# Squares made in the matmul slots, every second linear step on ScalarE, and the second half of an expert's weights prepared in its third slot

## The reference

```
ln(v)  = (v - mean(v)) / sqrt(var(v) + 1e-5)
si, sj = ctx @ W[:D], ctx @ W[D:]                       # one number per token each
x1     = x + tanh(g_xattn) * (0.6*sigmoid(si[:,None] + sj[None,:] + b) + 0.4*ln(x))
logits = ln(x1) @ wg                                    # 4096 tokens, 8 experts
e      = argmax(softmax(logits)); gate = softmax(logits)[e]
out    = x1 + tanh(g_ffn) * gate * (W[e] @ ln(x1) + b[e])
```

## Time and profile before

| | |
|---|---|
| median of three runs | 585.31 us |
| profiled execution, its own time | 590.49 us |
| its span | 588.7 us |
| granted TensorE clock, mean | 0.959 |
| PE / PEld / DVE / ACT / POOL busy | 538.2 / 448.9 / 406.4 / 277.3 / 336.1 us |
| first product of slot 0 | 160.16 us |
| first product of slot 2 | 188.09 us |
| last finish begins | 575.59 us |

### The profile page before, as it was taken

One profiled execution on the slowest core, in us unless ns is written; L12 is line 12 of the kernel. 1 busy time (PEld: TensorE's weight loads), 2 busy tenths in 40 slices (PEclk: granted clock), 3 DMA queues, 4 the chain that ended last, 5 costly groups with the idle time before them and its releaser, 6 DMA issues.

```text
span 588.7 us, 13585 instructions
## 1 busy us (share of the span) xinstructions
PE 538.2 (91%) x2770; PEld 448.9 (76%) x2771; DVE 406.4 (69%) x534; ACT 277.3 (47%) x408; POOL 336.1 (57%) x502
## 2 busy tenths in 40 slices
PE   8999988687797979989989999999999999999990
PEld 7888877576666858868868888888888888888880
DVE  1868858796898878946964895895598469733420
ACT  4689888688623434423433443443344234332220
POOL 2688888988743544456347336436644663474652
PEclk9699989899999989989989999999999999999996
DMA  7979885964987898786887689789678858564431
GB/s 258 384 250 264 289 313 176 334 214 154 360 318 179 249 270 224 238 242 204 251 249 240 180 241 256 224 242 257 221 221 236 260 154 243 145 212 144 139 117 36
DMA packets 84397, 135.21 MB, mean 230 GB/s; under 512 B 12048, under 2 KB 64784, under 8 KB 84368
## 3 DMA queue, kind: packets, MB, share of 16 engines
q1 hardware_dynamic: 68432, 81.88, 49.3%
q0 software_dynamic: 9792, 33.82, 15.3%
q10 hardware_dynamic: 6144, 19.18, 10.4%
HBM read 101.01 MB, written 35.93 MB: 233 GB/s over the span
## 4 chain that ended last, share of the span: by engine, by line
PE 52%; POOL 13%; DVE 12%; issue 10%; DMA 7%; ACT 2%; DVEq 1%; ACTq 1%; POOLq 1%; SPq 0%
PE pair L1265 47%; POOL table L544 5%; DVE wt L945 4%; POOL ln_b L530 2%; DVE pair L940 2%; DMA out_x<-rows,scatter_row 2%; PE pair L1199 2%; POOL xr_first L536 2%; DMA gates<-in_L_xattn_b 2%; PE pair L1187 2%; DVE rows L970 1%; DVE xr_first L893 1%; DVE xt L958 1%; DMA rows<-table 1%; POOL ln_r L521 1%
## 5 line engine op out<-in xcount | busy, mean ns | idle before, releaser
L1265 PE MATMUL pair<-wt,xt 128*128 (+1 forms) x1728 | 401.0, 394 | 14.0 <-DVE rows L970 9.6
L1265 PEld LDWEIGHTS pair<-wt,xt 128*128 128x128 f32 x1728 | 328.0, 190 | 86.0 <-issue 16.3
L708 ACT ACTIVATE wt<-pair 128x1024 f32 (+1 forms) x64 | 65.6, 1026 | 67.6 <-DVE pair L940 67.5
L590 POOL TENSOR_TENSOR rows<-rows,rb 128x1024 f32<-128x1024 f32 x37 | 89.2, 2409 | 12.5 <-ACT rb L781 11.8
L781 ACT ACTIVATE rb<-bias_bc,scal 128x1024 f32 (+1 forms) x37 | 46.0, 1245 | 77.2 <-POOL scal L585 61.9
L940 DVE STREAM_TRANSPOSE pair<-w_raw 128x1024 f32<-128x1024 f32 x64 | 79.7, 1249 | 1.4
L945 DVE TENSOR_TENSOR wt<-pair,wt 128x1024 f32 (+1 forms) x64 | 77.3, 1207 | 3.7 <-ACT wt L708 3.1
L594 POOL DMA_INDIRECT out_x<-rows,scatter_row x36 | 38.4, 1065 | 72.4 <-DVE rows L970 55.7
L958 DVE TENSOR_TENSOR xt<-pair,xt 128x1024 fp32r<-128x1024 f32 x38 | 46.5, 1225 | 42.5 <-ACT xt L714 42.4
L581 POOL TENSOR_TENSOR scal<-scal,minus_one 128x1 f32<-128x1 f32 x37 | 20.3, 549 | 90.9 <-ACT ez L773 90.9
L970 DVE SCALAR_TENSOR_TENSOR rows<-pair,scal,rows 128x1024 f32<-128x1024 f32 x36 | 46.2, 1283 | 34.2 <-PE pair L1265 34.1
(11 more groups left out here) (168 smaller groups left out, 422.8 us busy)
## 6 DMA issues: line engine op xcount, KB each, us to landing
w_raw<-in_L_ffn_W SPq DMA_DIRECT2D x256, 128.0 KB
xb<-table SPq DMA_DIRECT2D x156, 128.0 KB
rows<-table ACTq DMA_DIRECT2D x36, 520.0 KB
xr_first<-in_x SPq DMA_DIRECT2D x24, 512.0 KB, 9.2
ctx_in<-in_ctx SPq DMA_DIRECT2D x8, 512.0 KB, 8.4
bias_bc<-in_L_ffn_b SPq DMA_DIRECT2D x8, 512.0 KB, 5.4
xr_late<-in_x SPq DMA_DIRECT2D x4, 512.0 KB, 7.0
xr_last<-in_x SPq DMA_DIRECT2D x4, 512.0 KB, 8.6
```

What stands on the lines that cost most here:

```text
L590: nc.gpsimd.tensor_tensor(rows[:, k, 0:H], rows[:, k, 0:H], rb[:, :], ALU.add).then_inc(base_ready, 1)
L708: nc.scalar.activation(wt[:, bass.ds(place, 1), 0, :, P * m:P * (m + 1)].rearrange("p a k o -> p (a k) o"), ps[:, :].rearrange("p (k o) -> ...
L1265: last = nc.tensor.matmul(out_ps[r % 2][:, HALF * h:HALF * (h + 1)], xt[:, r % RING, x_part, k, :], wt[:, bass.ds(place + h, 1), w_part, k ...
```

## The change

- ACT's 32 squares leave the routing stage. Each slot squares its own rows behind the four `cut_high` and ahead of `exp_sum` (`square_sum`, 36 times in all, one ahead each, output `squares` or `th`); POOL's `slot_scalars` waits for it. `store` waits for `add_tanh` in place of the square.
- The linear step of odd tiles moves from POOL to ACT (`linear`, behind `half_tanh`).
- `choose` comes at the third tile of the next group and `position` and `rank` at the fourth; stores move behind them.
- The start of the routing stage is reordered: scalars of the first two tiles alone, statistics in another order, two sums of the context behind the first tile.
- An expert with four slots or more has its second half of weight work in the third slot (`fourth`). In a slot with weight work `finish` comes behind the third weight transpose.
- POOL's `add_base(t)` moves from the end of slot t-1 to the start of slot t. The load of slot 2's blocks and rows no longer waits for the table (their place is fixed).

```diff
             for s in range(RX):
                 sp.wait_ge(row_stored[s], stores_from(s))
+
+            load_blocks(sp, AHEAD * P, AHEAD)
             sp.wait_ge(rows_told, 1)
...
-            load_blocks(sp, row_of(2), 2)
...
             def linear(t):
+
                 s = slot_of(t)
                 pool.wait_ge(ln_b_ready, t + 1)
                 nc.gpsimd.tensor_scalar(row_at(s)[:, 0:H], row_at(s)[:, 0:H], ln_a[:, t:t + 1], ln_b[:, t:t + 1],
-                                        ALU.mult, ALU.add).then_inc(lin_ready, 1)
+                                        ALU.mult, ALU.add).then_inc(lin_even, 1)
...
-                pool.wait_ge(sq_ready, t + 1)
+                pool.wait_ge(xc_ready, t + 1)
...
-            norm_scalars(0)
+            norm_scalars(0, 0, 2)
             for t in range(2):
                 shift(t)
-                linear(t)
+                if t == 0:
+                    linear(t)
+            norm_scalars(0, 2, 2)
             for t in range(T):
                 g, r = t // GR, t % GR
                 if t + 2 < T:
                     shift(t + 2)
-                    linear(t + 2)
+                    if t % 2 == 0:
+                        linear(t + 2)
                 if r == 1 and g + 1 < NG:
                     norm_scalars(g + 1)
-                if r == 3 and g > 0:
-                    store(GR * (g - 1))
-                    store(GR * (g - 1) + 1)
-                if r < 2 and g > 1:
-                    store(GR * (g - 2) + 2 + r)
-            for t in range(T - GR - 2, T):
+                if r == 0 and g > 1:
+                    store(GR * (g - 2))
+                if r < 3 and g > 1:
+                    store(GR * (g - 2) + 1 + r)
+            for t in range(T - 2 * GR, T):
                 store(t)
 
             def slot_scalars(u, n, k, k2):
 
                 settled(rows_landed[k2], 16 * n + 16)
+                nc.gpsimd.tensor_scalar(scal[:, k, 1:2], rows[:, k, TH:TH + 1], c2h[:, 0:1], c2[:, 0:1],
+                                        ALU.mult, ALU.add).then_inc(mean_part, 1)
+                settled(sq_ready, u + 1)
                 nc.gpsimd.tensor_scalar(scal[:, k, 0:1], rows[:, k, SQ:SQ + 1], 1.0 / H, EPS,
                                         ALU.mult, ALU.add).then_inc(var_ready, 1)
-                nc.gpsimd.tensor_scalar(scal[:, k, 1:2], rows[:, k, TH:TH + 1], c2h[:, 0:1], c2[:, 0:1],
-                                        ALU.mult, ALU.add).then_inc(mean_part, 1)
...
             def slot(t, r, i):
+                add_base(t, r % RING)
                 slot_scalars(t + 1, RING * i + (r + 1) // 2, (r + 1) % RING, (r + 1) % 2)
 
                 settled(out_stored[r % 2], 16 * RING * i + 16 * (r // 2))
                 store_sums(t, r)
-                add_base(t + 1, (r + 1) % RING)
...
-            def square(t):
-                act.wait_ge(xc_ready, t + 1)
...
+            def linear(t):
+                row = row_at(slot_of(t))[:, 0:H]
+                act.wait_ge(ln_b_ready, t + 1)
+                nc.scalar.activation(row, row, ACT.Identity, bias=ln_b[:, t:t + 1],
+                                     scale=ln_a[:, t:t + 1]).then_inc(lin_odd, 1)
...
-
-                if t:
-                    square(t - 1)
                 copy_turned(t)
                 if t + RTH - 1 < T:
                     half_tanh(t + RTH - 1)
+                if t % 2 == 1 and t + 2 < T:
+                    linear(t + 2)
...
+            def square_sum(u, n, k, k2, where):
+
+                settled(rows_landed[k2], 16 * n + 16)
+                mine = rows[:, bass.ds(k, 1), :]
+                nc.scalar.activation(where, mine[:, :, 0:H].rearrange("p a h -> p (a h)"), ACT.Square,
+                                     accum_out=mine[:, :, SQ:SQ + 1].rearrange("p a h -> p (a h)")).then_inc(sq_ready, 1)
...
+            act.wait_ge(totalled, 1)
+            square_sum(2, 1, 2, 0, squares[:, :])
             exp_sum(2, 2)
...
                 after = (r + 1) % RING
+                square_sum(t + 1, RING * i + (r + 1) // 2, after, (r + 1) % 2, squares[:, :])
                 exp_sum(t + 1, after)
...
-                if r == 2 and g > 0:
+                if r == 3 and g > 0:
                     position(g - 1)
...
-                if r == 1 and g > 0:
+                if r == 2 and g > 0:
                     choose(g - 1)
...
+            nc.vector.memset(fourth[:, TAB - 3:TAB], 0.0)
+            nc.vector.tensor_scalar(fourth[:, 0:TAB - 3], nth[:, 3:TAB], 3.0, None, ALU.is_equal)
...
+            nc.vector.tensor_tensor(fourth[:, :], fourth[:, :], not_last[:, :], ALU.mult)
             link(nc.vector.tensor_tensor(kinds[:, :], not_last[:, :], used[:, :], ALU.add))
+            link(nc.vector.tensor_tensor(not_last[:, :], not_last[:, :], fourth[:, :], ALU.subtract))
+            link(nc.vector.scalar_tensor_tensor(out=kinds[:, 2:TAB], in0=fourth[:, 0:TAB - 2], scalar=2.0,
+                                                in1=kinds[:, 2:TAB], op0=ALU.mult, op1=ALU.add))
...
                             cut_low(n, m - 1, home, (cut_b, cut_a)[(m - 1) % 2])
+                        if m == WR - 2:
+
+                            finish(t, r, mine)
                     cut_low(n, WR - 1, home, cut_a)
                     settled(w_ready, WR * n + WR)
                 with dve.Else():
                     xt_low(t + 2, behind, cut_a)
-                finish(t, r, mine)
+                    finish(t, r, mine)
```

More of the change, by code:

```diff
@@ L80, in sem @@
             return st.enter_context(nc.semaphore(name))
-        ident = sb("ident", [P, P])
+        routing = ExitStack()
+        with routing:
+            ident = sb("ident", [P, P], F32, routing)
+            ones_bf = sb("ones_bf", [P, P], BF16, routing)
+            lower_bf = sb("lower_bf", [P, P], BF16, routing)
+            wg_sb = sb("wg_sb", [P, (K + 1) * GR * E - E], F32, routing)
+        squares = sb("squares", [P, H], BF16)
+        sb("gap_routing", [P, P + P + (K + 1) * GR * E - E - H // 2])
         eight_ones = sb("eight_ones", [P, E])
-        ones_bf = sb("ones_bf", [P, P], BF16)
-        lower_bf = sb("lower_bf", [P, P], BF16)
         gates = sb("gates", [P, 3])
@@ L167, in build @@
         end_by_slot = told[:, 0:TAB * E].rearrange("p (s e) -> p s e", e=E)
-        n_begun, newest, nth, base, not_last, used, kinds, first_base = [
-            told[:, TAB * (E + j):TAB * (E + j + 1)] for j in range(8)]
+        n_begun, newest, nth, base, not_last, used, kinds, first_base, fourth = [
+            told[:, TAB * (E + j):TAB * (E + j + 1)] for j in range(9)]
         rows = sb("rows", [P, RING, ROW])
@@ L511, in of_group, with norm_scalars @@
                 return rows_at(s, GR)[:, :, col:col + 1].rearrange("p r a -> p (r a)")
-            def norm_scalars(g):
-                four = slice(GR * g, GR * (g + 1))
-                pool.wait_ge(mv_ready, GR * (g + 1))
+            def norm_scalars(g, r=0, n=GR):
+                some, s = slice(GR * g + r, GR * g + r + n), slice(r, r + n)
+                pool.wait_ge(mv_ready, GR * g + r + n)
                 if g:
[L517 to L524, removed]
@@ L785, in table_of @@
                 return act.value_load(slot_tab[0:1, j, bass.ds(u, 1)], min_val=0, max_val=top)
+            for u in range(AHEAD):
+                act.wait_ge(xc_ready, T)
+                square_sum(u, 0, u, u, th[:, u, :])
             exp_sum(0, 0)
             scaled_bias(0, 0, 0, 0)
-            act.wait_ge(rows_told, 1)
             for s in range(RX):
                 act.wait_ge(row_stored[s], stores_from(s))
-            load_rows(act, table_of(2, 2, E * N - P), 2, 2)
+            load_rows(act, AHEAD * P, AHEAD, AHEAD)
             cut_high(2, 0, 2, cut_b)
@@ L972, in finish @@
                                                in1=row_of, op0=ALU.mult, op1=ALU.add).then_inc(finished, 1)
-            for t in range(LEAD):
+            for t in range(GR):
                 stats(t)
@@ L1237, in _ @@
                 turn_context(g)
-            for g in (2, 3):
-                sum_columns(g)
             pe.wait_ge(wg_landed, 16)
@@ L1245, in _ @@
                 turn_tile(t)
+                if t == 0:
+                    for early in (2, 3):
+                        sum_columns(early)
                 if r == 1 and g > 0:
                     logits_by_token(g - 1)
-                if r == 2 and g > 0:
+                if r == 3 and g > 0:
                     rank(g - 1)
-                if t == EARLY + GR - 1:
-                    pe.wait_ge(cum_ready, EARLY // GR + 1)
+                if t == EARLY + GR:
+                    pe.wait_ge(pos_ready, EARLY // GR)
                     nc.tensor.matmul(early_ps, ones_bf[:, :], cum[:, EARLY // GR % 2, 0:1],
```

51 lines of the change are left out of this document (33 added, 18 removed).

## The result

Before 585.07 us (584.69 to 587.78, 4 runs), after 601.73 us (600.11 to 603.16, 4 runs): ratio 1.0274, 95% interval 1.0230 to 1.0318, so slower by 2.7%. The forecast was 590.0 with a range of 568 to 602: the sign is right, the size 11.7 us short. The measured time lies just inside that range, and outside the forecast's own 583 to 597. One run of all that follow, 619.2 us of experiment 10, fell in a second, slower state of the device and counts in no comparison. The profiled execution took 603.16 us (span 601.4); before it was 590.49.

A forecast was written before the change was run, and what follows sets the result against it. Routing nearly fills all engines, its wait chain on POOL; in the slots ACT and POOL's loop overtakes PE. Last `finish` 7.0 us later, end 2.35 less: net +4.65 on 585.31 gives 590.0 us, range 568 to 602, the forecast's own 583 to 597.

The forecast's parts named there:

- The slot with weight work: ACT's slot from `rb` to `rb`: 12.73 us plus 1.65 for `finish` and 2.35 for the square makes 16.7.
- the square with its two POOL operations: Behind the last `cut_high`: square 1.05, read-out 0.1, POOL's variance and power 1.2; together 2.35 us, bounds 1.8 and 3.0.
- The slot behind it: Slot without weight work, its `rb` waiting for the output's store and the load of rows: 8.4 us.
- From `rb` of slot 2 to `rb` of slot 30: Slots: 12 pairs of 25.1 us, a weight slot and three more, 341.9 us in all.
- PE's waits: Slots: PE waits 1 to 2 us for `finish` in most slots, not three times for 3.
- The rival that they lower the clock: Slots: short waits lower PE's clock, a slot takes 12.8 us, 5 us more, 595 us; chance 0.13.
- The rival that the loop stays behind PE: Slots: PE keeps 10.86 us a slot, 557.7 us, or 571 with pairs of 23.5; chance 0.27.
- Routing: Routing stage: 8 us saved at 0.35 a tile and 1 at the start, together 9; bounds 2 and 15.
- The wait of DVE for POOL's linear step: Routing: odd tiles lose this wait altogether; at 0.8 us in every odd tile, routing would gain up to 13 us.
- Between the stages: Slot 2's block load no longer behind a table read: slot 2 begins 1.0 us earlier (0.5 to 1.5).
- The end: Kernel's end: the last `add_base`, for a slot that doesn't exist, was the last work; without it 2.35 us less.
- The base: Profiled execution 590.49 us, taken as 5.2 above the runs' median; net +4.65 added to the median 585.31.

The follow-up runs named there:

- experiment 10: Experiment 3's version, with ACT making `scaled_bias` before the load of rows in slots without weight work, code written out in both branches: 612.5 us, ratio 1.0403 to the kernel before.
- experiment 2: Changed kernel with `finish` of a slot with weight work back behind its last `cut_low`: 590.1 us, ratio 1.0043 to the kernel before.
- experiment 3: Changed kernel with the square of a slot with weight work moved between ACT's third and fourth `cut_high`: 576.0 us, ratio 0.9794 to the kernel before.
- experiment 1: Changed kernel with an expert's second half of weights turned in its second slot again: 600.4 us, ratio 1.0209 to the kernel before.
- experiment 6: Changed routing with the squares back on ACT in it; slots as before except `add_base`'s place: 587.4 us, ratio 1.0005 to the kernel before.
- 11: Changed kernel with squares left out of the slots, second half in the second slot, `finish` last: 583.5 us, ratio 0.9908 to the kernel before.
- experiment 7: Kernel before with only the second half of an expert's weights moved to its third slot: 583.6 us, ratio 0.9932 to the kernel before.
- experiment 12: Experiment 3's operations in the same order, with ACT's `exp_sum`, load and `scaled_bias` written out in both branches: 587.7 us, ratio 1.0029 to the kernel before.

## Why the prediction was right in its sign and short in its size

**The slot with weight work** was the term that decided the sign. Forecast 16.7, measured 16.5. Its parts: `finish` 1.65 forecast, 16.5 - 15.3 = 1.2 measured (experiment 2); the square with its two POOL operations 2.35 forecast, 16.5 - 13.9 = 2.6 measured (experiment 3). **The slot behind it**: forecast 8.4, measured 8.6 as the mean of thirteen (7.7 to 10.7; the longer ones wait for the rows' landing). From `rb` of slot 2 to `rb` of slot 30 forecast 341.9, measured 344.0, of which the first slot, at 18.2, is 1.7.

**PE's waits** came as forecast in kind, many short ones for `finish`, but 18 and not one in most slots. The rival that they lower the clock fell. The granted clock from 300 to 450 us was 1.00 (2.4 GHz), a lone slot of 48 took 11.14 to 11.20 us behind waits of 0.9 to 1.5 us. Only behind the two long waits was PE slower: 24.05 us for two slots behind 5.14, 35.92 for three behind 3.44, where two take 22.05 in experiment 3 and three 32.95 in experiment 1.

**The rival that the loop stays behind PE** fell by one placement. Experiment 3 shows that kernel: 576.0 us, where the prediction had 571 for pairs of 23.5.

**Routing.** Forecast 9 us, measured 8.1 against this execution of before, but that was luck, two wrong halves that cancel: 11.3 between the tiles instead of 8, and 3.2 lost at the start instead of 1 gained. And my reason was only half of it. I gave the gain to POOL's lost linear steps; experiment 6 shows that without the squares' leaving these bring nothing that can be told, since ACT is then full, and 11 against 6 that the squares' leaving brings 3.9 us. The wait of DVE for POOL's linear step, which I had gone from the odd tiles, is still there and has become more frequent: an even tile's linear step of POOL now runs beside the `add_tanh` of an odd one. Seven of the 32 `add_tanh` took 1.64 to 2.13 us, all of odd tiles, where before it was three (1.63, 1.92 and 2.08). Tile 7 (timeline of POOL and DVE):

```profile
50.65 1.19 POOL L550 TENSOR_SCALAR xr_first<-xr_first,ln_a,ln_b 128x1024 f32<-128x1024 f32 x1
50.78 2.13 DVE L921 SCALAR_TENSOR_TENSOR xr_first<-th,c,xr_first 128x1024 f32<-128x1024 f32 x1 [0.84 <-ACT xr_first L702]
```

**Between the stages.** Forecast 1.0 us gained, measured 1.1 lost: tile 31 8.1 us earlier, slot 2 only 7.0. The last table store was issued 7.6 us earlier (162.73, was 170.30). The load of the slot's blocks no longer waits for a table read, and yet it went out 7.9 us behind that store (170.66), where it was 7.6 with the read (177.89). What lies between that store and this load took as much longer as the read had taken; why, no run shows. The blocks had landed shortly before 177.11.

**The end** was a wrong step: the 2.35 us for the last `add_base` aren't there. Before, that operation ended at 581.25, 7.5 us before the span did. From the issue of the last store, 577.79, to the end of the span it was 10.9 us, and it is 10.8 now, so the end follows the store and not `add_base`. The store itself landed 2.8 us behind its issue in both traces; the 8 us behind that landing show no row of any engine, but for the rest of `add_base` before, and what fills them stays open. I had taken the last row of an engine for the last work.

**The base.** The profiled execution went from 590.49 to 603.16, +12.67, where the steps gave +4.65; between them lie 8.0, and to a tenth or two these are `rb` of slot 2 (194.4 for 191.3, 3.1), the slots to 30 (2.1), PE's last four (0.6) and the end (2.35). The medians went up by 16.7, because before's profiled execution lay 5.4 us above its median and after's 1.4. Experiment 7 shows where such a difference can sit: 4.2 us in the same routing code. The means say the same: tile 31 comes at 152.1 us in the two traces with the old routing and at 146.2 in the ten with the new one, 6 us apart. So part of the 8.1 us gained in routing was probably the slow routing of one execution. The number that carried the forecast from the profile to the median, a constant offset, was worth 4 us of its 11.7 us of error. How much of it is chance isn't settled: the kernel before took 585.1 in four runs beside the changed kernel, but 587.2 to 588.0 in 9 to 22 runs beside the experiments, and against those the median went up by 13.7 to 14.5 us and not by 16.7.

## What to carry to other kernels

An operation that is cheap and idle-time work by its engine's share can be the dearest of the change if it stands behind the last hand-over of a loop: the square cost 26 us behind the fourth `cut_high` and nothing that can be told in front of it. When two additions stretch one loop, time each alone but don't add the gains, since the next bound takes over. And read a gain in a stage against more than one execution of the old code before it goes into a forecast.

## What the runs showed of the hardware

**A loop whose code grows can start to be fetched again on each pass.** The packets of the queue "instruction" between 200 and 560 us, in experiments 3, 10 and 12:

```profile
q14 instruction: 6, 0.05, 0.1%
```

```profile
q14 instruction: 27, 0.22, 0.2%
```

```profile
q14 instruction: 31, 0.25, 0.3%
```

In experiment 3 all six came before 260 us, in experiment 12 some in every pass. In experiment 12 the five stalls of ACT for "issue" ahead of `xt_high` were 4.23, 4.02, 4.06, 4.34 and 4.00 us, 64 to 72 us apart, once in six slots, which is one pass of the loop. The profile shows them only as idle time that nothing ended. The Trainium skill, page "Runtime: NRT & Kernel Launch", section "Instruction fetch mechanics", says that a taken branch whose target lies outside the two pages that the engine's instruction memory holds must fetch the target's page before execution goes on. The traces agree: 4 us a pass, and no such stall in the loop of experiment 3.

**The start runs at the lower clock for longer.** From 30 to 40 us, the kernel after and before (columns as in the earlier trace rows):

```profile
30.00:40.00 10.00, 10.00 (x65) 8.26 (x64) 5.84 (x9) 5.52 (x8) 4.09 (x7) 0.74 0.74 251
```

```profile
30.00:40.00 10.00, 10.00 (x80) 8.66 (x79) 7.44 (x13) 8.58 (x14) 9.01 (x12) 0.93 0.72 249
```

PE is busy all the time in both and gets 65 instead of 80 matmuls through, at a granted clock of 0.74 for 0.93 (part of the time at 1.2 GHz, part at 2.4). Over 20 to 50 us the granted clock is 0.73 to 0.77 in all twelve traces with the new start, and tile 8's `add_tanh` comes at 54.1 to 55.9 us; it is 0.87 and 0.85 in the two with the old one (before and experiment 7), with tile 8 at 51.81 and 50.75. The delay of tile 8 first shows in a wait of DVE, 4.09 us ahead of tile 3's `add_tanh`. DVE waits there for ACT's linear step, which stands behind ACT's copy of a transposed tile, and PE makes that transpose behind two sums of the context: these took 3.41 and 3.55 us, and 2.29 and 1.93 before, for the same 16 matmuls each. The order of the start changed along with the clock, so how much is the clock's alone, and why it rises later, wasn't tried.
